# Where the attention stages keep their weights and partial sums, and how the weighting is split

## The reference, cut to what matters

```python
# layer 1, 4 heads of 64          (softmax over the edges of one node)
scores = einsum('ehd,ehd->eh', Q[dst], K[src] + 0.2 * rel[edge_type]) / 8
ex     = exp(scores - segment_max(scores, dst)[dst])
agg    = segment_sum(ex / segment_sum(ex, dst)[dst] * V[src], dst)
# layer 2, 8 heads of 32          (softmax over all edges)
alpha  = softmax((q[dst] * (k[src] + edge_attr @ We + be)).sum(-1) / sqrt(32), axis=0)
out    = segment_sum(v[src] * alpha, dst)
```

## Time and profile before

| | us |
|---|---|
| median of 3 runs | 4558.12 |
| the profiled execution, its own time | 4554.94 |
| its span, first to last instruction | 4553.1 |
| attend, layer 1, first L1751 to the end of its last quad | 805.7 |
| attend, layer 2, the same | 850.9 |
| busy: VectorE 3258.7 (72%), GpSimd 3148.8 (69%), TensorE 2757.1 (61%), ScalarE 720.5 (16%) | |

### The profile page before, as it was taken

One profiled execution on the slowest core, in us unless ns is written; L12 is line 12 of the kernel. 1 busy time (PEld: TensorE's weight loads), 2 busy tenths in 40 slices (PEclk: granted clock), 3 DMA queues, 4 the chain that ended last, 5 costly groups with the idle time before them and its releaser, 6 DMA issues. The chain is left out here.

```text
span 4553.1 us, 52726 instructions
## 1 busy us (share of the span) xinstructions
PE 2757.1 (61%) x11454; PEld 1449.6 (32%) x11454; DVE 3258.7 (72%) x7572; ACT 720.5 (16%) x2122; POOL 3148.8 (69%) x2929
## 2 busy tenths in 40 slices
PE   4245678888885997666566757687877763000006
PEld 4145322222222885222222334344443432000004
DVE  7498358888885333788889966588888886666664
ACT  0011100000000332333323321111111112000003
POOL 0577667767664776777777757677777764777772
PEclk8555799999998998788878778778788876555558
DMA  3235346666664332655555632456666652444441
GB/s 155 41 104 157 80 139 177 177 173 172 176 173 126 57 63 58 165 160 161 160 159 163 177 67 67 134 166 168 167 167 165 169 136 60 108 108 108 108 107 41
DMA packets 408930, 594.52 MB, mean 131 GB/s; under 512 B 267146, under 2 KB 273430, under 8 KB 407806
## 3 DMA queue, kind: packets, MB, share of 16 engines
q0 software_dynamic: 185552, 519.27, 41.5%
q1 hardware_dynamic: 223278, 74.01, 6.9%
HBM read 532.97 MB, written 59.26 MB: 130 GB/s over the span
## 5 line engine op out<-in xcount | busy, mean ns | idle before, releaser
L1690 PE MATMUL edge_psX<-state,ident 128*128 128x512 f32 x720 | 480.5, 804 | 217.9 <-DMA state<-tab,edge_feat 134.3
L1106 POOL DMA_INDIRECT edge_ring<-tab,edge_rec x480 | 469.8, 979 | 146.2 <-issue 135.6
L2016 POOL DMA_INDIRECT state<-tab,edge_rec x480 | 453.8, 945 | 155.0 <-issue 145.9
L1685 PE MATMUL edge_psX<-edge_w_edge,edge_featT 64*128 64x256 f32 x1920 | 446.2, 454 | 119.6 <-DVE edge_prod L1752 117.0
L1615 POOL DMA_INDIRECT state<-tab,edge_rec x360 | 419.7, 1166 | 130.0 <-issue 108.8
L1615 POOL DMA_INDIRECT state<-tab,edge_feat x360 | 393.8, 1094 | 109.7 <-issue 100.8
L1135 PE MATMUL edge_psX<-state,ident 128*128 x720 | 380.4, 638 | 140.0 <-DVE edge_ring L1163 140.0
L1685 PEld LDWEIGHTS edge_psX<-edge_w_edge,edge_featT 64*128 64x128 f32 x1920 | 300.3, 220 | 412.6 <-issue 353.1
L2189 PE MATMUL gate_psA<-ident,gate_w_nat 128*128 128x128 f32 x8 | 2.0, 428 | 631.4 <-DMA gate_w_nat<-in_L_gnn_W_ih 631.4
L1163 DVE TENSOR_TENSOR edge_ring<-edge_psX,edge_ring 128x1024 f32<-128x1024 f32 x240 | 293.8, 1224 | 73.8 <-PE edge_psX L1142 43.8
L781 POOL DMA_INDIRECT sorted_d<-update_row_out,update_row_idx x200 | 237.7, 1189 | 91.8 <-issue 60.0
(11 more groups left out here) (447 smaller groups left out, 6513.4 us busy)
## 6 DMA issues: line engine op xcount, KB each, us to landing
sorted_d<-state SPq DMA_DIRECT2D x7, 2380.0 KB
state<-src_rows SPq DMA_DIRECT2D x25, 562.5 KB
state<-low_rows SPq DMA_DIRECT2D x25, 562.5 KB
state<-tab,edge_rec POOLq DMA_INDIRECT x840, 3.0
edge_ring<-tab,edge_rec POOLq DMA_INDIRECT x600, 3.7
update_row_out<-in_edge_attr SPq DMA_DIRECT2D x40, 156.2 KB
edge_rec<-rec_d SPq DMA_DIRECT2D x364, 8.0 KB, 2.9
state<-tab,edge_feat POOLq DMA_INDIRECT x360
```

Of the source, the lines that this page charges most:

```text
L1106: pool.indirect_dma_start(out=ring[:, k, s, :], out_offset=None, in_=S["tab0"][:, :], in_offset=bass.IndirectOffsetOnAxis(ap=rec[:, k, R_S ...
L1685: pe.matmul(psX[k % 2][:, s % 2, s // 2, :], featT[lo:lo + ED, k % 4, s // PAIR, :], w_edge[lo:lo + ED, :], start=(s < 2), stop=False, ski ...
L1690: last = pe.matmul(psX[k % 2][:, a, :, :], S["ident"][:, :], ring[k % RING].rearrange("p (c a) f -> p a c f", a=2)[:, a, :, 0:D], start=Fa ...
L2016: pool.indirect_dma_start(out=ring[:, k, s, :], out_offset=None, in_=S["tab3"][:, :], in_offset=bass.IndirectOffsetOnAxis(ap=rec[:, k, R_S ...
```

## The change

The weights that ScalarE writes (`w`) move from the SBUF tile `wgt` with two halves to one PSUM bank, `psW`, without halves. The weighting of the four value rows, one instruction in place in the ring, becomes two instructions of two rows each: the first writes rows 0 and 1 to the other PSUM bank, `psS` (`first`), the second writes rows 2 and 3 to an SBUF tile `terms`. `halve` adds `first` to `terms`. The rescaled `acc` goes to `so_far`, the first 256 columns of the same bank `psS`; the two rows of `terms` are added to it one after the other, the first in PSUM, the second into `acc`. The slot of the ring is freed behind `halve`. The mask now waits for `halve`, and the first of the two additions waits for the rescaling (`decay`). The number of marked instructions per quad goes from 12 to 13.

```diff
-        wgt = ph.sb("wgt", [P, 2, ROWS, heads])
+        terms = ph.sb("terms", [P, 2, D])
+        psW, psS = (ph.ps(n, [P, 512]) for n in ("psW", "psS"))
+        w = psW[:, 0:ROWS * heads].rearrange("p (r h) -> p r h", h=heads)
+        so_far = psS[:, 0:D]
+        first = psS[:, :].rearrange("p (s d) -> p s d", d=D)
-        CH = 12 * AQ
+        CH = 13 * AQ
-                        act.activation(wgt[:, k % 2, :, :], cat[:, k % 2, :, :], ACT.Exp).then_inc(s_exp, 1)
+                        act.activation(w, cat[:, k % 2, :, :], ACT.Exp).then_inc(s_exp, 1)
+                def weigh(at, h):
+                    vals = ring[at][:, 2 * h:2 * h + 2, D:D2].rearrange("p s (h d) -> p s h d", h=heads)
+                    to = terms[:, :, :] if h else first
+                    return dve.tensor_tensor(to.rearrange("p s (h d) -> p s h d", h=heads), vals,
+                                             bc(w[:, 2 * h:2 * h + 2, :], 3, [P, 2, heads, hd]), ALU.mult)
+                def halve():
+                    return dve.tensor_tensor(terms[:, :, :], terms[:, :, :], first, ALU.add)
+                def decay(acc):
+                    return dve.tensor_tensor(so_far.rearrange("p (h d) -> p h d", h=heads), acc.rearrange("p (h d) -> p h d", h=heads),
+                                             bc(w[:, QE, :], 2, [P, heads, hd]), ALU.mult)
+                def add_half(to, i):
+                    return dve.tensor_tensor(to, so_far, terms[:, i, :], ALU.add)
...
                         step.put(dve.tensor_tensor(l, l, w[:, QE, :], ALU.mult))
-                        weighted = step.put(dve.tensor_tensor(vals, vals, bc(w[:, 0:QE, :], 3, [P, QE, heads, hd]), ALU.mult))
+                        step.put(weigh(at, 0))
+                        weighted = step.put(weigh(at, 1))
                         dve.wait_ge(s_xr, t * AQ + (k + 3))
...
                         step.until(weighted)
-                        halved = step.put(dve.tensor_tensor(v[:, 0:2, :], v[:, 0:2, :], v[:, 2:4, :], ALU.add))
-                        step.until(scored)
+                        halved = step.put(halve())
+                        dve.nop().then_inc(s_done[at], 1)
+                        step.until(halved)
                         masked = step.put(dve.tensor_tensor(score[:, 0:QE, :], score[:, 0:QE, :], bc(mask, 2, [P, QE, heads]), ALU.add))
-                        step.put(dve.tensor_tensor(acc_h, acc_h, bc(w[:, QE, :], 2, [P, heads, hd]), ALU.mult))
+                        decayed = step.put(decay(acc))
                         step.until(masked)
                         dve.nop(nofuse=True)
                         highest = step.put(dve.tensor_reduce(m, score.rearrange("p r h -> p h r"), AX.X, ALU.max))
-                        step.until(halved)
-                        summed = step.put(dve.tensor_tensor(v[:, 0, :], v[:, 0, :], v[:, 1, :], ALU.add))
+                        step.until(decayed)
+                        summed = step.put(add_half(so_far, 0))
...
                         step.until(summed)
-                        step(dve.tensor_tensor(acc, acc, v[:, 0, :], ALU.add))
-                        dve.nop().then_inc(s_done[at], 1)
+                        step(add_half(acc, 1))
```

More of the change, by code:

```diff
@@ L1703, in last_values @@
                 def last_values(step, t, k, at, b):
                     dve.wait_ge(s_exp, t * AQ + (k + 1))
-                    w = wgt[:, at % 2, :, :]
-                    v = ring[at][:, :, D:D2]
                     acc = blk(S["big"], b)[:, D:D2]
-                    acc_h = acc.rearrange("p (h d) -> p h d", h=heads)
                     l = blk(S["l"], b)[:, 0:heads]
-                    vals = v.rearrange("p s (h d) -> p s h d", h=heads)
                     dve.nop(nofuse=True)
                     dve.tensor_tensor(l, l, w[:, QE, :], ALU.mult)
-                    dve.tensor_tensor(vals, vals, bc(w[:, 0:QE, :], 3, [P, QE, heads, hd]), ALU.mult)
+                    step.put(weigh(at, 0))
@@ L1715, in last_values @@
+                    step.put(weigh(at, 1))
                     step(dve.tensor_reduce(tot[:, :], w[:, 0:QE, :].rearrange("p r h -> p h r"), AX.X, ALU.add))
-                    step(dve.tensor_tensor(v[:, 0:2, :], v[:, 0:2, :], v[:, 2:4, :], ALU.add))
-                    dve.tensor_tensor(acc_h, acc_h, bc(w[:, QE, :], 2, [P, heads, hd]), ALU.mult)
                     dve.tensor_tensor(l, l, tot[:, :], ALU.add)
-                    step(dve.tensor_tensor(v[:, 0, :], v[:, 0, :], v[:, 1, :], ALU.add))
@@ L1720, in last_values @@
-                    step(dve.tensor_tensor(acc, acc, v[:, 0, :], ALU.add))
+                    step(halve())
+                    step(decay(acc))
+                    step(add_half(so_far, 0))
+                    step(add_half(acc, 1))
                     dve.nop().then_inc(s_done[at], 1)
@@ L1728, in _ @@
                 pre(dve.memset(ring[RING - 1][:, :, D:D2], 0.0))
-                pre(dve.memset(wgt[:, 1, 0:QE, :], 0.0))
-                pre(dve.memset(wgt[:, 1, QE, :], 1.0))
+                pre(dve.memset(w[:, 0:QE, :], 0.0))
+                pre(dve.memset(w[:, QE, :], 1.0))
                 if layer == 1:
@@ L1746, in _ @@
                         score, m = cat[:, k % 2, :, :], blk(S["m"], b)[:, 0:heads]
-                        w, v = wgt[:, at % 2, :, :], ring[at][:, :, D:D2]
                         acc, l = blk(S["big"], b_prev)[:, D:D2], blk(S["l"], b_prev)[:, 0:heads]
-                        acc_h, vals = acc.rearrange("p (h d) -> p h d", h=heads), v.rearrange("p s (h d) -> p s h d", h=heads)
                         dve.wait_ge(s_x, t * AQ + (k + 1))
```

## The result

| | before | after |
|---|---|---|
| median of 4 runs, us | 4557.5 (4555.3 to 4558.4) | 4444.95 (4443.6 to 4447.8) |
| ratio to before | | 0.9753, 95% interval 0.9741 to 0.9765 |
| profiled execution (span) | 4554.9 (4553.1) | 4445.8 (4444.0) |
| forecast | | 4491 (4448 to 4540) |

The account below looks back on a forecast made before the run. GpSimd's descriptor lists, delayed by VectorE instructions with two SBUF inputs, were taken as the bound. 125 us of waits saved less 58 us of VectorE growth made 67 us less: 4491 us, range 4448 to 4540.

Parts of the forecast that it names:

- The mechanism: Both attends: GpSimd lists wait for VectorE instructions with two SBUF inputs, 101 us in layer 2, 96 plus 9 in layer 1.
- The gain in waits: VectorE's waits in both attends: 80 of 88 us go in layer 2, 45 of 54 in layer 1, together 125.
- The growth of VectorE's chain: Each quad of both attends grows by 0.24 us, bounds 0.08 and 0.65; 58 us over 240 quads.
- The marker: Slot-free marker moved from the quad's idle end to behind the halving: -0.02 us per quad, 0 to -0.06.
- The split: Two weightings of 512 elements for one of 1024: +0.10 us per quad, at most 0.25.
- PSUM operands: Eight VectorE instructions of a quad get a PSUM operand: nothing to 0.01 us each, +0.04 in all.
- The mask's wait: The mask must wait for the halving: +0.11 us per quad, upper bound 0.33.
- The rescaling's wait: The first addition waits for the rescaling, which has all but ended by then: +0.01 us per quad.
- A: The VectorE reduction also holds GpSimd up, 0.5 us per quad: gain 57 us, 4501 us; chance 0.12.
- B: TensorE at its low clock bounds layer 2, half of that layer's gain goes: 4531 us; chance 0.10.
- C: Waits between dependent VectorE instructions cost 0.33 us each, chain +0.78 us per quad: 62 us slower, 4620; chance 0.07.
- D: Any VectorE instruction streaming SBUF for long holds GpSimd up, both layers stay at its pace: 4564 us; chance 0.05.

Follow-up runs that it names:

- w3: Kernel before with only the weights moved to PSUM (one buffer, no halves), weighting and sums still in SBUF: 4436.3 us, ratio 0.9731.
- w1: Changed kernel with the weights back in one SBUF tile, sums still in PSUM and weighting still split: 4461.2 us, ratio 0.9788.
- w2: Changed kernel with the slot's marker back behind the last addition of a quad: 4473.0 us, ratio 0.9812.
- v10: Kernel before with only the weights in PSUM, plus the in-place weighting split into two instructions of two rows: ratio 1.0158, total not usable.
- w4: Changed kernel with halving ahead of the weights' total, the mask not waiting for it, the rescaling waiting instead: 4424.5 us, ratio 0.9704.
- u9: Kernel before with a quad's last addition and marker waited for beside the next quad, not at its end: ratio 0.9966, total not usable.

## Why the forecast was right in kind and 45 us too small

**What bounds the kernel: right.** The forecast said that GpSimd's lists filled the window of layer 2 and drove the waits of layer 1, though VectorE looked the busiest. w3 shows it: almost the same chain on VectorE, bare lists beside the weighting, 121 us less. One step of the argument is looser than it reads: the nine lists that are missing from the 600 ran ahead of the window. Inside it GpSimd works for 839 us of 851, its last list ends at 3732.36, 13 us before the window does, and that is as good as full.

**The mechanism: right.** Lists fell to 0.946 us where "below 0.98" was to show it, and both long two-input instructions turn out responsible on their own: moving one operand of L1756 ended its delays and left the halving's (w3); leaving only the weights in SBUF brought some back (w1). The Trainium skill (page "SBUF — State Buffer", section "Who interferes with whom") says that a VectorE instruction with two SBUF inputs contends with a GpSimd instruction that reads SBUF, and one with at most one SBUF input does not; the lists here behave so. The same section infers that making descriptors isn't held up by a `tensor_tensor`; the 209 lists that lost 0.64 us each say otherwise, and the measurement decides. It also says that issue order decides who blocks; the sharp border in w1 fits that, but it lies some 0.02 to 0.03 us behind the start of VectorE's instruction and not at it.

**The gain in waits: right within 3 us.** 142 us of waits were there by the forecast (143 by the count used here), 17 were to stay. What stayed is 11.7 us in layer 1 (9 forecast) and 3.7 in layer 2 (8 forecast), 15.4 in all (from the first quad to the last are 766.8 and 764.7 us, less 119 quads and 14 starts of a turn, 2.0 us each). In layer 1 it is one stall for the exponential in the first turn and little else; "the stall dies out within two or three turns" was too careful by one or two:

```profile
1875.12 0.16 DVE L1770 TENSOR_TENSOR l<-l,edge_psW 128x4 f32 x1 [9.45 <-ACT edge_psW L1665]
```

**The growth of VectorE's chain: the step that failed.** +0.24 us per quad was forecast, bounds 0.08 and 0.65; +0.08 and +0.05 were measured, so 120 x 0.13 = 16 us and not 58. That is 42 of the 45 us; the waits are the other 3. In the sum +0.10 + 0.11 + 0.01 + 0.04 - 0.02 three terms were mis-sized, the marker's most:

- The marker: -0.12 us and not -0.02 (bound -0.06); 24 us. The forecast gave no row for the 0.02. The 0.26 us of idle time in the earlier trace rows was there to be split into a wait and a marker; edge_mlp's wait without a marker stood beside it: 0.73 us from start to start, 0.69 long, so 0.04 us idle. The gap of 0.26 against 0.04 was a clue, and the forecast used both numbers only as the ends of the mask's wait. The marker is only part of that gap: with it away 0.15 us stay idle. w2 shows the term.
- The split: +0.06 and not +0.10; 10 us. The 0.62 us came from an L1763 that had a list beside it (the row at 3306.96 above); undisturbed it is 0.60, in w3 as in each of the two weightings. From 1.24 against 1.13 it went to 1.20 against 1.14. v10 shows +0.07 for the split alone.
- PSUM operands: +0.04 forecast. What moved in layer 2 outside the other terms, mask to rescaling up by 0.02 and the rest down by as much, sums to nothing; 10 us. Whether the 0.02 at the rescaling comes of its output in PSUM or of the wait ahead of the mask was not separated. The rule that an instruction with a PSUM source pays 62 cycles more (the Trainium skill, "VectorE: DVE Perf Modes", errata table), priced at 125 us in the prediction, does not hold here: in w3 the weighting of 1024 elements takes 1.21 us with its weights in PSUM, against 1.22 before with both inputs in SBUF.
- The mask's wait: right. +0.10 in layer 2 and +0.08 in layer 1 by the rows before and after, +0.11 against the undisturbed halving of 0.60 us, and w4 shows it. The rescaling's wait: nothing in layer 2 and 0.03 in layer 1 (maximum to first addition), against +0.01.

In layer 2 the missing 0.19 us per quad are the marker (0.10), the split (0.04), the operands (0.04) and the two waits (0.01 each), to rounding; in layer 1 0.16 are missing. 120 x (0.19 + 0.16) = 42 us.

One number in the list of signs doesn't follow from the sum: an attend 1 of about 779 us. 752 us for VectorE alone, 9 of waits and 120 x 0.24 make 790; with the 800 of layer 2 that is the forecast's 67 us. Measured were 772.9 and 771.3.

**The rivals.** A (the reduction holds lists up too) is false: 178 lists have their step inside L1774, up to 1.11 us into it, and lose 0.003 us on average. B (TensorE becomes the bound) is false: VectorE waits 5 times for it, two of these at the start of a layer, and the granted clock went up. C (each wait costs 0.33 us) is false: the mask's costs 0.11, and the rescaling's 0.03 at most; of the 0.34 us at the end of a quad 0.12 are the marker. D (no effect) is false: lists fell to 0.946 us. The range reached up to B and down to 4448; its lower end held one small term from its own lower bound, when three of them (marker, split, operands) came out low at once.

## What to carry to other kernels

Beside indirect DMAs that GpSimd issues, and where GpSimd sets the pace, give a long VectorE `tensor_tensor` at most one SBUF input. Where several instructions share a small operand, put that into PSUM first and measure before going on: here 32 elements per partition brought 121 us by themselves, and the rest of the change was gains (fewer waits, the marker) and costs (the split, the mask's wait) that cancelled. Look at the length of single lists and at what VectorE runs 0.12 us after their start, not at busy shares: the busiest engine was not the bound. When an engine's chain has become the bound, put semaphore markers beside running work (0.12 us each at an idle end), and order small independent work into waits (0.10 us each). Read the price of a step from a quad without a list beside it.

## What the runs showed of the hardware

- A `nop` that carries a semaphore increment costs VectorE 0.12 us behind a completed wait (0.56 to 0.68 us from last addition to score copy, w2), and nothing visible behind a running instruction (0.71 us from halving to mask with and without it).
- A VectorE instruction that doesn't wait begins 0.07 to 0.09 us ahead of the end of the one before it; the mask that waits for the halving begins 0.03 to 0.04 us behind its end. The price of that wait is the 0.11 us between 0.60 and 0.71. At the end of a quad a wait costs 0.22 us (0.34 against 0.56, u9 and the changed kernel).
- The exclusion of lists and two-input instructions works both ways. A list that starts 0.04 us or more behind a 128x512 instruction loses up to 0.53 us; one that starts with it (0.00 or 0.01 us) is on time, and VectorE's instruction takes 0.72 to 0.75 us instead of 0.69 (w1).
- A short two-input instruction costs lists less: mean lists in layer 1 take 1.17 us beside weightings of 1.22 us (before) and 1.00 beside those of 0.69 (w1).
